# Decoder with routed experts: one shared-expert group ahead of the block loop instead of two, and the token list made behind that group

## The chip, the cores and the metric

The kernel runs on one core of a Trainium2 chip. The metric is the device time of one execution in microseconds (us); lower is better. It is given as the median of several executions.

## What is computed

A two-layer decoder on 16 sequences of 128 tokens and 512 features, in float32. The change lies in its last part alone, the mixture of experts of layer 1, on 2048 tokens (cut from the reference):

```python
scores = softmax(xt @ Wg.T)                    # 16 experts in 4 groups
... top 2 groups by their maximum, then top 4 experts of those: topi, weights
combine = zeros((T, E)).at[arange(T)[:, None], topi].add(weights)
h = silu(einsum('td,eid->eti', xt, W1)) * einsum('td,eid->eti', xt, W3)   # INTER = 352
y = einsum('etd,te->td', einsum('eti,edi->etd', h, W2), combine)
z = silu(xt @ Ws1.T) * (xt @ Ws3.T) @ Ws2.T    # shared expert, 704 wide, for every token
out = _layernorm(x + y + z)
```

## The kernel before

The stage is `build_experts` (from L2088). Its work, in TensorE's order:

1. The tokens are transposed (L2425), router logits are formed (L2431, L2436), and VectorE picks four experts for each token.
2. **Shared groups ahead.** The shared expert z goes by four groups of four sequences (512 tokens). One group is `shared_ups` (six chunks of 128 hidden features, each with a gate tile "sg" and an up tile "su": L2403, 96 matmul records) and then `shared_downs` (four tiles "sy" of 12 records: L2416, 48 records). ScalarE makes the gate (L2370), VectorE the product `hs` (`shared_hidden`, L2610), and VectorE adds the four results to y (`shared_add`, L2617). Groups 0 and 1 (`EARLY`) run here. In the middle of group 0 two small products give each pair of token and expert its rank (L2445, L2446), and VectorE computes the slots from it.
3. **The token list.** 80 slots of blocks hold 128 tokens each, one expert to a block. For each of a token's four choices k, VectorE writes one-hot marks (`mark(k)`, L2671, L2674 and twice L2677) into one of two buffers (`at_row` lies in `back`, `at_block` in the weight buffer of expert 1). TensorE multiplies them (`list_products`, L2454, 16 products for each k, all added up in one bank). `mark(2)` and `mark(3)` write over the buffers of k = 0 and k = 1, and so wait for `list_taken`, which the products of k = 0 and k = 1 raise. `list_out` (L2686 to L2693) turns the bank into token numbers: after its first copy it raises `list_taken` to 4, for which SyncE waits before it loads the weights of expert 1 (L2261, L2262), and its last instruction lets GpSimd copy one column of numbers (L2316) and gather the 128 token rows of block 0 and then of block 1 by an indirect DMA (L2319).
   In the kernel before, the marks of k = 0 and 1 are made by VectorE during the downs of group 0; their products stand behind chunk 2 of group 1, those of k = 2 and 3 behind chunk 4 of it.
4. **The block loop.** TensorE first waits until all early shared results are added (`s_added`) and the rows of block 0 are there (`gathered`), transposes them (`turn(0)`, L2473), and then runs 79 blocks: transpose, gate product (L2483), hidden transpose (L2478), up product (L2483), down product (L2490). ScalarE's `yrow` is stored to DRAM.
5. **Shared groups behind.** Groups 2 and 3 (`LATE`) follow the loop. Beside them GpSimd gathers the 64 tiles of expert results (four for each of 16 sequences, L2335) and VectorE adds them up, weighted (`combine_one`, L2752): up to five behind each chunk's `hs` and one behind each `shared_add`. The normalisation's sums (`sums`, L2760) of sequences 0 to 11 are made in `combine_one` when the fourth result of a sequence is added; `moments_of(0)` follows chunk 3 of the last group, and sequences 0 to 11 are normalised between the additions of the last group (L2771), then the last four.

Each engine runs its instructions strictly in this written order. `Tiles` hands out the eight PSUM banks in the order of the list `order`; a tile can start once the tile eight places earlier has been read.

Of the kernel before, what the change touches and what calls it, by code (L numbers as in the profile page):

```python
# [31 lines left out]
GB = SEQS // GROUPS  # L32
# [2057 lines left out]
def build_experts(nc, t, chunk_in, home):  # L2090
# [10 lines left out]
    with ExitStack() as ctx:  # L2101
# [9 lines left out]
        NGR, TOPG, TOPK = 4, 2, 4  # L2111
# [6 lines left out]
        NI, NS = len(inner), len(shared)  # L2118
# [117 lines left out]
                "sy": lambda: (s_added, GB * n[0] + n[1] + 1),  # L2236
            }[kind]()

        EARLY, LATE = (0, 1), (2, 3)
        early = shared_tiles(EARLY)  # L2240
        RANK_AT = NS // 2
        TURNED = [*range(GB, SEQS), *range(1, GB), 0]
        ROUTED = [*range(1, GROUPS), 0]
        order = [("xt", b) for b in TURNED] + [("rl", g) for g in ROUTED] + [("rt",)]
        LISTED = {2: (0, 1), 4: (2, 3)}
        list_at = early.index(("sg", EARLY[1], min(LISTED) + 1))
        order += early[:2 * RANK_AT] + [("rank",)] + early[2 * RANK_AT:list_at] + [("list",)] + early[list_at:]

        READY = (range(0, SEQS - GB), range(SEQS - GB, SEQS))
        first = Tiles(banks, semaphore("filled"), order, drained)  # L2250
# [146 lines left out]
        def _(pe):  # L2397
# [9 lines left out]
            def shared_ups(tiles, g, chunks=range(NS)):  # L2407
                for c in chunks:
                    up(tiles, ("sg", g, c), ws1, shared[c], g)
                    up(tiles, ("su", g, c), ws3, shared[c], g)  # L2410

            def shared_downs(tiles, g):
                for b in range(GB):
                    bank = tiles.start(pe, 0, ("sy", g, b), [(s_h, NS * (g + 1))])
                    for c in range(NS):
                        ins = pe.matmul(bank[:, :], hs[:, c, b * P:(b + 1) * P], ws2[:, c, :],  # L2416
                                        start=(c == 0), stop=(c == NS - 1))
                    tiles.done(ins)
# [31 lines left out]
            def list_products(ks):  # L2450
                for k in ks:
                    pe.wait_ge(list_marked.sem, k + 1)
                    for b in range(SEQS):
                        ins = pe.matmul(bank[:, 0:2 * LIST], at_row[:, k % 2, b, :],  # L2454
                                        at_block[:, k % 2, b].rearrange("p i j -> p (i j)"),
                                        start=(k == 0 and b == 0), stop=(k == TOPK - 1 and b == SEQS - 1))
                    if k < TOPK - 1:
                        ins.then_inc(list_taken.sem, 1)
                    else:
                        first.done(ins)  # L2460

            for c in range(NS):
                shared_ups(first, EARLY[1], range(c, c + 1))
                if c in LISTED:
                    if 0 in LISTED[c]:
                        bank = first.start(pe, 0, ("list",))
                    list_products(LISTED[c])
            shared_downs(first, EARLY[1])

            def turn(v):  # L2470

# [69 lines left out]
        def _(dve):  # L2541
# [64 lines left out]
            def shared_hidden(tiles, g, c):  # L2606
                n, m = NS * g + c, shared[c][1]
                bank = tiles.wait(dve, 0, ("su", g, c))
                dve.wait_ge(s_gated.sem, n + 1)
                dve.tensor_tensor(hs[0:m, c, :], bank[0:m, :], gated[0:m, n % 2, :], ALU.mult).then_inc(s_h.sem, 1)  # L2610

            def shared_add(tiles, g, b):
                bank = tiles.wait(dve, 0, ("sy", g, b))
                s = GB * g + b
                if s in added:
                    dve.wait_ge(added[s][0].sem, added[s][1])
                dve.tensor_tensor(y[:, s, :], bank[:, :], y[:, s, :], ALU.add).then_inc(s_added.sem, 1)  # L2617
                added[s] = (s_added, s + 1)
# [48 lines left out]
            def mark(k):  # L2667

                if k >= 2:
                    dve.wait_ge(list_taken.sem, k - 1)  # L2670
                vstep.did(dve.tensor_tensor(at_row[:, k % 2], restf[:, k, :].unsqueeze(2).broadcast_to([P, SEQS, P]),  # L2671
                                            columns_of.unsqueeze(1).broadcast_to([P, SEQS, P]), ALU.is_equal))
                one = at_block[:, k % 2, :, 0, :]
                chained(dve.tensor_tensor(one, quotf[:, k, :].unsqueeze(2).broadcast_to([P, SEQS, LIST]),  # L2674
                                          columns_of[:, 0:LIST].unsqueeze(1).broadcast_to([P, SEQS, LIST]), ALU.is_equal))
                for i in (1, 0):
                    ins = dve.tensor_tensor(at_block[:, k % 2, :, i, :], one,  # L2677
                                            marks[:, i, :].unsqueeze(2).broadcast_to([P, SEQS, LIST]), ALU.mult)
                    if i:
                        chained(ins)  # L2680
                ins.then_inc(list_marked.sem, 1)
# [15 lines left out]
            dve.sem_inc(hid_ready.sem, AHEAD)  # L2697
            for c in range(RANK_AT, NS):
                shared_hidden(first, EARLY[0], c)
            for k in LISTED[2]:  # L2700
                mark(k)
            for b in range(GB):
                shared_add(first, EARLY[0], b)
            for c in range(3):
                shared_hidden(first, EARLY[1], c)
            for k in LISTED[4]:
                mark(k)
            for c in range(3, 5):
                shared_hidden(first, EARLY[1], c)
            list_out()  # L2710
            for c in range(5, NS):
                shared_hidden(first, EARLY[1], c)
            for b in range(GB):
                shared_add(first, EARLY[1], b)

            def columns(v):

# [29 lines left out]
            def combine_one():  # L2747
                n, b, k = combine.pop(0)
                dve.wait_ge(returned[n % SLOTS].sem, 16 * (n // SLOTS + 1))
                if b in added:  # L2750
                    dve.wait_ge(added[b][0].sem, added[b][1])
                add_to_y(b, dve.scalar_tensor_tensor(y[:, b, :], back[:, n % SLOTS], top[:, b, k:k + 1], y[:, b, :],  # L2752
                                                     ALU.mult, ALU.add))
                if b in READY[0] and k == TOPK - 1:
                    sums(b)

            def sums(b):

                dve.wait_ge(added[b][0].sem, added[b][1])
                vstep.did(dve.bn_stats(stats[:, b, :], y[:, b, :]))  # L2760
# [13 lines left out]
            for g in LATE:  # L2774
                for c in range(NS):
                    shared_hidden(last, g, c)
                    for _ in range(min(5, len(combine))):
                        combine_one()
                    if g == LATE[-1] and c == NS - 3:
                        moments_of(0)  # L2780
                for b in range(GB):
                    shared_add(last, g, b)
                    if combine:
                        combine_one()
                    if g == LATE[-1]:
                        normalise(0, READY[0][b * len(READY[0]) // GB:(b + 1) * len(READY[0]) // GB])
# [144 lines left out]
```

## Time and profile before

| | us |
|---|---|
| median of 3 runs | 2826.8 (2824.01 to 2828.55) |
| profiled execution | 2823.79, its span 2822.0 |
| TensorE busy in the span | 2639.3 (94%) |
| experts stage begins (first record of L2425) | 1880.5 |
| last TensorE record ends | 2811.4 |

Times below count from the start of the profiled span. A row of the timeline or the chain gives start, duration, engine, line and what is written from what. For TensorE one float32 product of the program leaves two matmul records.

### The profile page before, as it was taken

The numbers are of one execution on the slowest core, as the hardware profiler recorded it, in microseconds if no ns is written. First come the engines' busy times: TensorE is split into PE (matmuls) and PEld (weight loads), VectorE is DVE, ScalarE is ACT, GpSimd is POOL, SyncE is SP. The second block draws the span as 40 slices with busy tenths as digits, with TensorE's granted clock in tenths as the row PEclk, the third lists the DMA queues.
The fourth block names the chain that finished last, engine by engine and source line by source line (L and its number), as shares of the span: only waits on it lengthen the run. The fifth ranks groups of instructions, "written<-read, shape, count | busy, mean of one in ns | idle before, by whom it ended". The sixth has DMA issues, their size and how long they took to land. (4 is left out here: it accounts for less than half of the span.)

```text
span 2822.0 us, 33590 instructions
## 1 busy us (share of the span) xinstructions
PE 2639.3 (94%) x10940; PEld 1330.5 (47%) x10941; DVE 1388.7 (49%) x2555; ACT 839.3 (30%) x1896; POOL 527.3 (19%) x564
## 2 busy tenths in 40 slices
PE   8999999999999958799999999859999999999998
PEld 4544554555465433344344344224456656665543
DVE  4546564564557262567777777607322222222255
ACT  2324332442342232145455455530011111111101
POOL 2111101110111001333233233000011111111054
PEclk9999999999999988899999999979999999999999
DMA  6120122122202301434454454340123333332155
GB/s 197 60 75 30 66 70 90 60 63 86 76 31 75 116 1 61 79 75 104 106 112 103 105 116 98 100 168 0 43 95 130 129 128 126 113 144 97 53 145 160
DMA packets 108316, 260.04 MB, mean 92 GB/s; under 512 B 19523, under 2 KB 53059, under 8 KB 96675
## 3 DMA queue, kind: packets, MB, share of 16 engines
q1 hardware_dynamic: 95490, 219.87, 26.2%
q0 software_dynamic: 11440, 37.50, 4.5%
q8 instruction: 71, 1.16, 0.2%
q10 hardware_dynamic: 1264, 1.10, 0.1%
q14 instruction: 51, 0.41, 0.1%
HBM read 203.14 MB, written 54.89 MB: 91 GB/s over the span
## 5 line engine op out<-in xcount | busy, mean ns | idle before, releaser
L2483 PE MATMUL d_bank<-d_w,d_xcol 128*128 x1264 | 401.3, 461 | 0.0
L2019 DVE TENSOR_REDUCE c_mx<-c_pair 128x2 f32<-128x1024 f32 x256 | 303.5, 1217 | 109.3 <-PE c_pair L1879 108.3
L1728 ACT ACTIVATE c_probs<-c_exp 128x512 f32<-128x512 f32 x512 | 277.9, 597 | 217.0 <-PE c_exp L1893 213.8
L2483 PEld LDWEIGHTS d_bank<-d_w,d_xcol 128*128 128x128 f32 x1264 | 229.0, 191 | 101.0 <-issue 1.4
L796 PE MATMUL a_bank<-h_quarters,a_ring 128*128 128x512 f32 x608 | 272.9, 600 | 0.0
L547 POOL TENSOR_TENSOR a_ry<-a_rt 128x512 f32<-128x512 f32 x80 | 130.3, 1629 | 759.6 <-DVE a_rt L1048 759.6
L796 PE MATMUL a_bank<-a_wo,h_rows 128*128 128x512 f32 x512 | 222.4, 593 | 0.0
L2490 PE MATMUL d_bank<-d_w,d_hid 128*128 x480 | 219.2, 593 | 0.7 <-DVE d_hid L2721 0.7
L1851 PE MATMUL c_step<-h_quarters,c_xT 128*128 128x512 f32 x384 | 185.7, 608 | 7.9 <-DVE c_r L2012 3.8
L1893 PE MATMUL c_exp<-c_qs,c_ks 128*128 128x512 bf16 x512 | 160.5, 384 | 19.5 <-ACT c_probs L1728 11.6
L796 PEld LDWEIGHTS a_bank<-h_quarters,a_ring 128*128 128x128 f32 x608 | 115.0, 193 | 132.3 <-issue 129.6
L2403 PE MATMUL d_bank<-d_xT,d_ws 128*128 128x512 f32 (+1 forms) x384 | 166.7, 594 | 0.7 <-ACT d_yrow L2380 0.7
L2380 ACT ACTIVATE d_yrow<-d_bank 128x512 f32<-128x512 f32 x80 | 47.8, 597 | 380.1 <-PE d_bank L2490 380.1
L796 PEld LDWEIGHTS a_bank<-a_wo,h_rows 128*128 128x128 f32 x512 | 97.4, 190 | 120.9 <-issue 120.4
L2718 DVE COPY d_xcol<-d_bank 128x512 f32<-128x512 f32 x79 | 54.6, 691 | 188.8 <-PE d_bank L2473 188.8
L1879 PE MATMUL c_pair<-c_ks,c_qs 96*128 96x512 bf16 x512 | 142.8, 384 | 3.5 <-DVE c_mx L2019 3.4
L1903 PE MATMUL c_pv<-c_probs,c_vt 128*32 128x512 f32 x1024 | 138.0, 611 | 0.7 <-ACT c_probs L1728 0.7
L2490 PEld LDWEIGHTS d_bank<-d_w,d_hid 128*128 128x128 f32 x480 | 91.3, 190 | 94.0 <-issue 76.4
L585 ACT ACTIVATE a_ee<-a_ry 128x512 f32<-128x512 f32 x80 | 50.8, 635 | 272.3 <-POOL a_ry L547 272.3
L2316 POOL COPY d_index<-d_tokens 128x1 uint32 (+1 forms) x79 | 14.3, 181 | 614.2 <-DVE d_xcol L2718 488.2
L2721 DVE COPY d_hid<-d_bank 128x384 f32<-128x384 f32 x80 | 44.6, 558 | 164.5 <-PE d_bank L2478 164.5
L1851 PEld LDWEIGHTS c_step<-h_quarters,c_xT 128*128 128x128 f32 x384 | 69.5, 191 | 102.2 <-issue 96.0
(305 smaller groups left out, 3559.6 us busy)
## 6 DMA issues: line engine op xcount, KB each, us to landing
d_w<-in_w SPq DMA_DIRECT2D x16, 1408.0 KB
scratch_results<-d_yrow SPq DMA_DIRECT2D x80, 256.0 KB
a_ring<-in_wq SPq DMA_DIRECT2D x16, 1024.0 KB, 4.8
a_wo<-in_wo SPq DMA_DIRECT2D x16, 1024.0 KB, 4.8
c_ks<-scratch_kpark SPq DMA_DIRECT2D x96, 128.0 KB, 4.3
c_qs<-scratch_qpark SPq DMA_DIRECT2D x96, 128.0 KB, 4.3
d_w<-in_w SPq DMA_DIRECT2D x16, 768.0 KB
a_ring<-in_w SPq DMA_DIRECT2D x8, 1024.0 KB, 7.9
```

The lines of the kernel that those rows point to most:

```text
L547: pool.tensor_tensor(ry[:, n % 2, :], rt1[:, n % 2, :], rt2[:, n % 2, :], ALU.add).then_inc(rope_sum.sem, 1)
L796: ins = pe.matmul(bank[:, :], lhs(c), rhs(c), start=(c == 0), stop=(c == n - 1))
L1728: act.activation(probs[:, (LC * CH * n + k) % RING, :], bank[:, :], ACT.Exp, scale=float(CD) ** -0.5).then_inc(exped.sem, 1)
L1851: ins = pe.matmul(bank[:, :], rows[:, c, :], w[:, c, :], start=(c == 0), stop=(c == KC - 1))
L1879: ins = pe.matmul(bank[:, 512 * i:512 * i + 512], qs[0:TR, n % STACKS, h, at0:at0 + P], ks[0:TR, n % STACKS, h, :], start=True, stop=True)
L1893: exps.done(pe.matmul(bank[:, :], ks[:, n % STACKS, h, l * P:(l + 1) * P], qs[:, n % STACKS, h, :], start=True, stop=True))
L1903: ins = pe.matmul(pv[32 * j:32 * j + 32, :], head_values(n, q, l, j), probs[:, (LC * CH * n + QUAD * m + j) % RING, :], start=(l == 0), st ...
L2019: dve.tensor_reduce(mx[:, n % 2, at0:at0 + 2], bank[:, :].rearrange("p (i n) -> p i n", i=2), AX.X, ALU.max).then_inc(maxed.sem, 1)
L2403: ins = pe.matmul(bank[0:m, :], w[:, c, c0:c0 + m], xT[:, c, GT * group:GT * (group + 1)], start=(c == 0), stop=(c == KC - 1))
L2483: ins = pe.matmul(bank[:, 0:FI], xcol[:, v, k, :], w13[:, bass.ds(at, 1), which, k, :].rearrange("p a n -> p (a n)"), start=(k == 0), stop ...
L2490: ins = pe.matmul(bank[:, :], hid[:, v, c * P:(c + 1) * P], w2[:, bass.ds(at, 1), c, :].rearrange("p a n -> p (a n)"), start=(c == 0), sto ...
L2718: dve.tensor_copy(xcol[:, v].rearrange("p c n -> p (c n)"), turned_bank[:, :]).then_inc(xcol_ready.sem, 1)
```

## The change

`EARLY` becomes group 0 alone and `LATE` becomes groups 1, 2 and 3. TensorE makes all four `list_products` in a row, directly behind the downs of group 0. VectorE makes the four marks in a row as well, with the additions of group 0's results behind marks 2 and 3 and behind `list_out`. The sums of sequences 0 to 11 leave `combine_one` and are made in the last late group, four sequences behind each of its first three chunks.

```diff
-        EARLY, LATE = (0, 1), (2, 3)
+        EARLY, LATE = (0,), (1, 2, 3)
...
-        LISTED = {2: (0, 1), 4: (2, 3)}
-        list_at = early.index(("sg", EARLY[1], min(LISTED) + 1))
-        order += early[:2 * RANK_AT] + [("rank",)] + early[2 * RANK_AT:list_at] + [("list",)] + early[list_at:]
+        order += early[:2 * RANK_AT] + [("rank",)] + early[2 * RANK_AT:] + [("list",)]
...
-            for c in range(NS):
-                shared_ups(first, EARLY[1], range(c, c + 1))
-                if c in LISTED:
-                    if 0 in LISTED[c]:
-                        bank = first.start(pe, 0, ("list",))
-                    list_products(LISTED[c])
-            shared_downs(first, EARLY[1])
+            bank = first.start(pe, 0, ("list",))
+            list_products(range(TOPK))
...
-            for k in LISTED[2]:
-                mark(k)
             for b in range(GB):
+                mark(b)
+                if b >= 2:
+                    shared_add(first, EARLY[0], b - 2)
+            list_out()
+            for b in range(2, GB):
                 shared_add(first, EARLY[0], b)
-            for c in range(3):
-                shared_hidden(first, EARLY[1], c)
-            for k in LISTED[4]:
-                mark(k)
-            for c in range(3, 5):
-                shared_hidden(first, EARLY[1], c)
-            list_out()
-            for c in range(5, NS):
-                shared_hidden(first, EARLY[1], c)
-            for b in range(GB):
-                shared_add(first, EARLY[1], b)
...
-                if b in READY[0] and k == TOPK - 1:
-                    sums(b)
...
+                    if g == LATE[-1] and c < NS - 3:
+                        for b in range(GB * c, GB * c + GB):
+                            sums(b)
```

## Rows read from the trace of the kernel before

**Rows 1.** The chain that ended last, around the early groups: start, us, what.
```profile
1948.11 20.87 PE d_bank L2416 x48
1968.97 20.60 PE d_bank L2403 x48
1989.57 2.30 PE d_bank L2454 x32
2005.65 2.30 PE d_bank L2454 x32
2036.63 0.70 DVE h_quarters L2617
2037.38 0.67 PE d_bank L2473 x4
2041.04 1.11 PE d_bank L2473 x4
2042.15 3.41 PE d_bank L2483 x8
...
2050.83 0.44 PE d_bank L2473 x4
...
2058.91 0.44 PE d_bank L2473 x4
```

**Rows 2.** TensorE's timeline behind the block loop.
```profile
2684.94 41.61 PE L2403 MATMUL d_bank<-d_xT,d_ws 128*128 128x512 f32 x96 [0.69 <-ACT d_yrow L2380]
2727.48 20.87 PE L2416 MATMUL d_bank<-h_rows,d_hs 128*128 128x512 f32 x48 [0.93 <-DVE d_hs L2610]
2748.19 41.51 PE L2403 MATMUL d_bank<-d_xT,d_ws 128*128 128x512 f32 x96
2790.54 20.87 PE L2416 MATMUL d_bank<-h_rows,d_hs 128*128 128x512 f32 x48 [0.84 <-DVE d_hs L2610]
```

**Rows 3.** VectorE's timeline: marks 0 and 2, next mark, additions, `list_out`.
```profile
1947.98 2.27 DVE L2671 TENSOR_TENSOR d_back<-d_restf,d_spots 128x2048 bf16<-128x2048 f32 x1
...
1961.38 1.28 DVE L2617 TENSOR_TENSOR h_quarters<-d_bank,h_quarters 128x512 f32<-128x512 f32 x2
...
1990.76 2.29 DVE L2671 TENSOR_TENSOR d_back<-d_restf,d_spots 128x2048 bf16<-128x2048 f32 x1 [0.46 <-PE d_bank L2454]
...
1994.51 3.05 DVE L2677 TENSOR_TENSOR d_w<-d_w,d_spots 128x1296 bf16<-128x1296 bf16 x2
1997.48 2.28 DVE L2671 TENSOR_TENSOR d_back<-d_restf,d_spots 128x2048 bf16<-128x2048 f32 x1
...
2007.98 0.69 DVE L2610 TENSOR_TENSOR d_hs<-d_bank,d_gated 128x512 f32<-128x512 f32 x1 [3.11 <-PE d_bank L2454]
2008.59 0.32 DVE L2686 COPY d_listed<-d_bank 128x162 f32<-128x162 f32 x1
```

**Rows 4.** The timeline of GpSimd and of SyncE's queue at the token list.
```profile
2008.99 0.34 SPq L2261 DMA_DIRECT2D d_w<-in_w  x1
...
2011.33 1.15 POOL L2319 DMA_INDIRECT d_xrow<-scratch_x,d_index  x1 [0.91 <-POOL d_index L2316]
```

**Rows 5.** The gathers of token rows: all 79, then the first alone.
```profile
DMA to landing us min/median/max: 3.2/3.4/7.8
...
DMA to landing us min/median/max: 6.1/6.1/6.1
```

**Rows 6.** Stretches: us, busy time of each engine, granted clock, DMA share, GB/s.
```profile
1870.00:1880.00 10.00, 0.00 (x0) 0.00 (x0) 2.98 (x7) 0.50 (x2) 0.00 (x0) 0.50 0.14 54
2040.00:2042.00 2.00, 0.96 (x5) 0.96 (x6) 0.00 (x0) 0.00 (x0) 0.95 (x1) 0.68 0.19 41
2042.00:2044.00 2.00, 2.00 (x5) 1.25 (x5) 0.69 (x1) 0.00 (x0) 0.18 (x1) 0.50 0.25 90
2044.00:2046.00 2.00, 2.00 (x9) 1.28 (x9) 0.07 (x1) 0.31 (x1) 0.97 (x1) 0.97 0.07 12
2016.00:2017.00 1.00, 1.00 (x3) 0.41 (x3) 0.00 (x0) 0.00 (x0) 0.00 (x0) 1.00 1.01 399
```

**Rows 7.** VectorE's timeline at the end: last combination, closing sums, normalisation.
```profile
2795.78 0.75 DVE L2752 SCALAR_TENSOR_TENSOR h_quarters<-d_back,d_top,h_quarters 128x512 f32<-128x512 f32 x1 [0.55 <-DMA d_back<-scratch_results,d_row_no]
...
2813.41 2.46 DVE L2760 BATCH_NORM_STATS2 d_stats<-h_quarters 128x6 f32<-128x512 f32 x4
...
2816.89 1.91 DVE L2771 TENSOR_SCALAR h_quarters<-h_quarters,d_mom,d_rstd 128x512 f32<-128x512 f32 x4 [0.60 <-ACT d_rstd L2359]
```

## The prediction

> **What bounds the kernel now.** I read the busy times, then the chain of work that ended last in the experts stage, then the timelines of the engines around it. The reader should see in the chain [rows 1] that from the downs of group 0 (1948.11) to the first block nearly every piece is TensorE's, each starting where the last one ends. The token list costs TensorE only its two runs of products (2.30 us each); all that VectorE, GpSimd and the DMA do for it lies beside group 1. Behind the loop [rows 2] it is the same: from 2684.94 TensorE stands still only for 0.93 and 0.84 us, ahead of the downs. So a shared group costs about its TensorE time wherever it stands, and the question is what it covers there. Ahead of the loop it covers the making of the token list. Behind the loop it covers the 64 combinations, and those are covered with two groups already: the last one starts at 2795.78 [rows 7], and TensorE works until 2811.4 [rows 2].
>
> **What is moved at no cost or gain.** The products, marks, additions, gathers and weight loads are the same in number before and after. Group 1 leaves the front with the TensorE time that it brings to the back. The sums of 12 sequences leave the combinations and come, four at a time, behind three chunks of the last group, where the combinations are now finished: the combinations need 64 places, 34 of which (6 x 5 + 4) are in the first late group and 30 in the second. Four sums are 2.46 us [rows 7], and a chunk's TensorE time is 41.5/6 = 6.9 us [rows 2], which hides them; without that cover the 12 would cost 7.4 us. VectorE is freer by as much in the first two late groups, and the two waits of 0.93 and 0.84 us may shrink to the 0.77 us that hs alone needs (41.61 from 2684.94 to 2726.55 is followed by one hs of 0.69 and two handovers): at most 0.2 us, taken as nothing. The end is the same chain as before: last downs, last addition, four sums, moments, normalisation, 10.6 us from TensorE's end to 2822.0. The third late group doesn't touch it, because these four sequences belong to the last group in both kernels.
>
> **What is added at the back.** One more group. The distance from one late group to the next is 2748.19 - 2684.94 = 63.25 us [rows 2], with its wait. TensorE is the bound in it: **+63.25**.
>
> **What is taken from the front.** Before, from the end of the downs of group 0 (1968.97) to turn(0) (2037.38) there are 68.4 us [rows 1]. They go. In their place stands the list's own chain, now bare. I follow it step by step.
> - TensorE starts the products of k = 0 at 1968.97. The products stand behind the downs in its order, though marks 0 and 1 have been ready since 1961.4 [rows 3].
> - VectorE stands at mark(2), which waits for the buffer of k = 0. Queued behind it are the additions of group 0, mark(3) and list_out, and all of GpSimd's and SyncE's next work waits for those. Before, mark(2) began 1.19 us after the products began (1989.57 to 1990.76) [rows 1, 3]. So it begins at 1970.16.
> - A mark takes 6.72 us to the next start (1990.76 to 1997.48), 6.80 to the end of its last part (1994.51 + 3.05) [rows 3]. Behind mark(2) comes one addition, half of the distance that two took (0.6 to 0.65 us; 0.60 taken). mark(3) then begins at 1977.48 and ends at 1984.28. Products of k = 2 run beside it.
> - TensorE has been idle from 1971.3 but for the products of k = 2. In the idle stretch 1870 to 1880 the granted clock was 0.50, that is the level of 1.2 GHz; at 2040 to 2042, after four microseconds with almost nothing since 2036.6, it was falling (0.68), and at 2042 to 2044, with work again, 0.50 [rows 6]. So the products of k = 3 are taken at half speed: 16 of the 32 that took 2.30 us are 1.15 at the full clock, 2.30 at half [rows 1]. With the handover list_out starts at 1986.66. At the full clock it would be 1985.5.
> - From list_out's first copy (2008.59) to the start of the first gather (2011.33) were 2.74 us, and the gather landed 6.1 us after that (2017.43) [rows 3 to 5]: 8.84 us together. So block 0 is there at 1995.50. Additions 2 and 3 (1.3 us) are done beside this.
> - The landing needs a choice. The median gather took 3.4 us, the longest 7.8 [rows 5]. The first was issued 2.34 us after the load of expert 1 (2008.99) [rows 4], and while it was under way the DMA engines were fully busy (1.01, 399 GB/s) [rows 6]. The change keeps load and gather in the same order and distance, so I take 6.1 and keep 3.4 and 7.8 for the range.
> - On that last point the Trainium skill ("DMA: Bandwidth & Descriptors", section "Issuing engines are not separate DMA queues") says that DMAs issued by SyncE and by GpSimd run on the same 16 engines and interleave. The trace agrees: 6.1 beside the full load, 3.4 as the median. By queues of their own the sum would be 2.7 us lower.
>
> turn(0) begins at about 1995.54, where it began at 2037.38: **-41.84**. It runs at the low clock: 1.11 against 0.67 us, as the transposes at 2041.04 [rows 1], **+0.44**. From turn(0) to the next transposes were 3.66 us before, most of it loop entry; block 1 lands close behind block 0 and doesn't hold them. The first products of the loop were slow before too (3.41 against 2.37), behind a pause of 4 us, so nothing more is added for them. The upper bound is a first block wholly at half speed: blocks are 8.08 us apart (2050.83 to 2058.91), the first took 9.79 (2041.04 to 2050.83) [rows 1], and twice 8.08 is 6.4 more than that.
>
> **Sum.** 63.25 - 41.84 + 0.44 = **+21.85 us**. The same from the other side: TensorE is idle from 1971.3 to 1995.5, 24.2 us, less 2 or 3 us of products within, less the 0.8 us that it stood before turn(0) before, plus the slow pieces. On the profiled execution 2823.79 + 21.85 = 2845.6. The median of the three runs is 3.0 us above the profiled execution, so for a median I take 2826.8 + 21.85 = **2848.7 us**, 0.8% slower.
>
> **The rivals.**
> - *The gather isn't hindered, or the clock holds.* A landing of 3.4 instead of 6.1 is -2.7, the products at full clock -1.15, turn(0) at full clock -0.44: 2844.4. Against it: rows 5 and 6.
> - *The chain is longer.* A gather of 7.8 (+1.7) and a first block wholly at the lower clock (+6.4): 2856.8. For it: the pause is 24 us instead of 5, and nothing in this stage shows one so long ahead of the loop. Against it: at 2044 to 2046 the granted clock is back at 0.97 after some 3 us of work.
> - *The change doesn't leave mark(2) waiting*, the four marks run through under the downs of group 0, as "in a row" would have it. Then the marks end at 1947.98 + 4 x 6.7 + 0.6 = 1975.4 instead of 1984.3: 2839.8. Against it: mark(2) waits for products that TensorE has behind the downs, so the order in the code excludes it. It would need products earlier in the queue.
> - *Not slower: the stream of results back (GpSimd's gathers and VectorE's combinations) is the bound behind the loop*, not TensorE. Then the third group fills time that is there anyway, its 63.25 us aren't paid, and only the -41.4 of the front is left: about 2785. The chain of waits does pass through GpSimd and DMA between 2695 and 2727, which speaks for it. Against it: the stream is done at 2796.5, 111.6 us after 2684.94, and two groups of TensorE alone are 126.5. It decides from the point at which the stream is longer than the TensorE time beside it: for a sum of zero 22 of the 63 us would have to be hidden, so it would have to end 22 us or more behind the two groups, and it ends 15 us ahead.
>
> **How the numbers follow.** Forecast 0.78; unhindered gather or full clock 0.07; longer chain 0.09; marks without a wait 0.02; stream as the bound 0.02; 0.02 for what none of these names. The range runs from the second case's 2844.4, less most of the spread of the executions (the lowest lay 2.8 us under the median), up to the larger of the third's two parts, 2848.7 + 6.4 = 2855.1: 2842.0 to 2855.0. A measurement of this kernel can tell about 0.2% (5.7 us) from no change. Slower by more than that needs +5.7, and every case but the stream gives +13 or more: slower 0.96, within 0.2% 0.02, faster 0.02.
>
> **What would show it.** In the profile after: products of L2454 in one stretch directly behind the first 48 records of L2416, with two pauses in which VectorE's L2671, L2674 and L2677 run (mark(2) beginning near 1970.2, mark(3) near 1977.5); list_out near 1986.7; a first L2473 near 1995.5; granted clock 0.5 in between; three late groups at a distance of 63.2 us, and 10.6 us from TensorE's end to the span's. The prediction is wrong if TensorE's pause ahead of turn(0) isn't 20 to 26 us in all, or if the third late group costs less than its 63 us, which would mean that something other than TensorE was the bound behind the loop.

## The result: 0.6% slower

| | before | changed |
|---|---|---|
| median of 4 runs | 2826.31 us | 2844.81 us (2840.32 to 2846.01) |
| ratio, with its 95% interval | | 1.0064 (1.005 to 1.0079) |
| profiled execution, its span | 2823.79, 2822.0 | 2845.80, 2844.0 |

The forecast was 2848.7 us, in a range of 2842 to 2855. In the profile after, L2401 is the line of the shared ups, L2414 of the downs, L2452 of the list products, L2466 of the token transposes and L2476 of the gate and up products. The marks are L2664, L2667 and L2670, `list_out` begins at L2679.

The chain that ended last in the changed kernel, from the downs of group 0 to the second block (start, us, what). It answers to [rows 1].

```profile
1947.48 20.87 PE d_bank L2414 x48
1968.35 1.16 PE d_bank L2452 x16
1969.51 0.02 issue
1969.53 2.29 DVE d_back L2664
...
1976.34 0.60 DVE h_quarters L2610
1976.93 2.20 DVE d_back L2664
...
1982.13 1.52 DVE d_w L2670
1983.66 0.05 issue
1983.70 2.36 PE d_bank L2452 x16
1986.06 0.02 issue
1986.08 0.34 DVE d_listed L2679
...
1988.83 5.83 DMA d_xrow<-scratch_x,d_index
1994.66 0.14 issue
1994.80 1.10 PE d_bank L2466 x4
...
1998.87 1.11 PE d_bank L2466 x4
1999.98 4.40 PE d_bank L2476 x8
...
2009.65 0.44 PE d_bank L2466 x4
```

Where [rows 1] showed TensorE without a break, the chain now leaves it for VectorE (marks of k = 2 and 3), comes back for one run of products, and goes out again through `list_out` and the gather's DMA. The stretch from the end of the downs (1968.35) to turn(0) (1994.80) is 26.45 us; before it was 68.4 us, with group 1 in it.

TensorE's waits in the experts stage of the changed kernel (who waited for whom: us in total, times, longest):

```profile
PE d_bank L2452 <- DVE d_w L2670: 10.7, 2, 5.8
PE d_bank L2466 <- DMA d_xrow<-scratch_x,d_index: 8.8, 1, 8.8
```

These two rows don't exist before the change. They are 19.5 us of TensorE standing still. The two pauses for the marks, in TensorE's timeline (the first row of products, those of k = 0 and 1, begins at 1968.18 without a wait):

```profile
1976.39 2.34 PE L2452 MATMUL d_bank<-d_w,d_back 128*128 128x162 bf16 x16 [5.75 <-DVE d_w L2670]
1983.70 2.34 PE L2452 MATMUL d_bank<-d_w,d_back 128*128 128x162 bf16 x16 [4.97 <-DVE d_w L2670]
```

TensorE's timeline behind the loop of the changed kernel, which answers to [rows 2]:

```profile
2643.76 41.61 PE L2401 MATMUL d_bank<-d_xT,d_ws 128*128 128x512 f32 x96 [0.69 <-ACT d_yrow L2378]
2686.57 20.87 PE L2414 MATMUL d_bank<-h_rows,d_hs 128*128 128x512 f32 x48 [1.20 <-DVE d_hs L2603]
2707.28 41.51 PE L2401 MATMUL d_bank<-d_xT,d_ws 128*128 128x512 f32 x96
...
2770.26 41.51 PE L2401 MATMUL d_bank<-d_xT,d_ws 128*128 128x512 f32 x96
```

Three groups at distances of 63.52 and 62.98 us. Within them TensorE waits only ahead of the downs (1.20, 0.78 and 0.78 us). The last TensorE record ends at 2833.4, and the span 10.6 us later, as before.

**A measure that is finer than the whole time.** The executions of one kernel spread by 5 to 16 us, and the layers ahead of the experts alone spread by 14: in the 13 profiles of this study the first shared products start anywhere from 1895.6 to 1910.0, with the same instructions ahead of them. The experts stage repeats much better: 939.77 and 939.03 us in two profiles of the changed kernel, and A and B of the kernel before came out the same to 0.01 us in e5, whose edit touches only C. One part of B repeats less well, the first block (see below). So the experiments are read by three stretches of their profiled executions: A from the first shared products to turn(0), B from turn(0) to the first late group (the loop), and C from there to the end of the span.

| kernel | A | B | C | sum | against before | median | ratio to before, 95% interval |
|---|---|---|---|---|---|---|---|
| before | 132.52 | 647.56 | 137.06 | 917.14 | | 2826.31 | |
| changed | 90.57 | 648.96 | 200.24 | 939.77 | +22.6 | 2844.81 | 1.0064 (1.005 to 1.0079) |
| e0 changed, once more | 90.67 | 648.35 | 200.01 | 939.03 | +21.9 | 2848.22 | 1.0077 (1.0062 to 1.0092) |
| e1 buffer for each mark | 80.91 | 648.62 | 199.98 | 929.51 | +12.4 | 2836.15 | 1.0034 (1.0022 to 1.0047) |
| e2 load behind gathers | 88.21 | 648.27 | 199.85 | 936.33 | +19.2 | 2844.84 | 1.0062 (1.0047 to 1.0078) |
| e3 filler products | 89.69 | 646.04 | 200.26 | 935.99 | +18.9 | 2844.66 | 1.0065 (1.0049 to 1.0081) |
| e9 = e1 and e2 | 79.18 | 648.88 | 200.16 | 928.22 | +11.1 | 2834.73 | 1.0032 (1.0021 to 1.0044) |
| e4 list early, sums moved | 147.14 | 648.82 | 143.32 | 939.28 | +22.1 | 2843.37 | 1.0072 (1.0054 to 1.009) |
| e5 sums moved alone | 132.52 | 647.57 | 142.53 | 922.62 | +5.5 | 2828.63 | 1.0019 (1.0008 to 1.0031) |
| e10 list early alone | 147.01 | 648.77 | 136.79 | 932.57 | +15.4 | 2833.99 | 1.005 (1.0034 to 1.0066) |
| e6 one late group | 195.50 | 648.43 | 122.01 | 965.94 | +48.8 | 2872.17 | 1.018 (1.0159 to 1.0201) |
| e7 late wait | 130.83 | 647.75 | 135.14 | 913.72 | -3.4 | 2820.11 | 0.9983 (0.9972 to 0.9994) |
| e8 late wait, turn(0) early | 133.47 | 642.40 | 135.15 | 911.02 | -6.1 | 2817.81 | 0.9973 (0.9962 to 0.9984) |

(In e8 A ends at turn(1), since turn(0) stands inside the downs; by the same mark the kernel before has A 136.18 and B 643.90. Each ratio is to runs of the kernel before made beside that kernel; their medians were 2821.7 to 2827.7 us. The edits shift the lines of the program, so each profile's rows carry the line numbers of its own kernel.)

### The profile page after: what moved, and what is told of

It is laid out like the page before. It is cut to its first block and busy times, and to the rows that moved or that the text cites. A ratio compares the mean times of both kernels' runs of the same rounds, so it can differ in the third digit from the quotient of the medians.

```text
span 2844.0 us, 33531 instructions
## 1 busy us (share of the span) xinstructions
PE 2634.7 (93%) x10881; PEld 1330.1 (47%) x10941; DVE 1386.2 (49%) x2555; ACT 838.6 (29%) x1896; POOL 528.7 (19%) x564
## 3 DMA queue, kind: packets, MB, share of 16 engines
q8 instruction: 71, 1.16, 0.2%
## 5 line engine op out<-in xcount | busy, mean ns | idle before, releaser
L2476 PE MATMUL d_bank<-d_w,d_xcol 128*128 x1264 | 402.2, 461 | 0.0
L2476 PEld LDWEIGHTS d_bank<-d_w,d_xcol 128*128 128x128 f32 x1264 | 229.0, 191 | 101.6 <-issue 2.0
L1893 PE MATMUL c_exp<-c_qs,c_ks 128*128 128x512 bf16 x453 | 147.2, 383 | 26.6 <-ACT c_probs L1728 12.3
L2401 PE MATMUL d_bank<-d_xT,d_ws 128*128 128x512 f32 (+1 forms) x384 | 166.4, 593 | 0.7 <-ACT d_yrow L2378 0.7
```

The costliest lines, as they stand in the source:

```text
L1893: exps.done(pe.matmul(bank[:, :], ks[:, n % STACKS, h, l * P:(l + 1) * P], qs[:, n % STACKS, h, :], start=True, stop=True))
L2401: ins = pe.matmul(bank[0:m, :], w[:, c, c0:c0 + m], xT[:, c, GT * group:GT * (group + 1)], start=(c == 0), stop=(c == KC - 1))
L2476: ins = pe.matmul(bank[:, 0:FI], xcol[:, v, k, :], w13[:, bass.ds(at, 1), which, k, :].rearrange("p a n -> p (a n)"), start=(k == 0), stop ...
```

## The experiments

Two theories were set against each other. A: the cost is the token list's chain, which now stands bare in front of TensorE. B: the cost lies behind the loop, where a third group stands beside the stream of results back. (The letters of the theories have nothing to do with those of the stretches.)

**e0, the base.**

> The changed kernel once more, beside the three variants of it on the same chip, as their base. Expected 1.0064 of the kernel before again (about 2844.5 us), and in the profile some 26.5 us from the end of the downs of group 0 to turn(0).

Measured: 1.0077, and 26.6 us from the end of the downs of group 0 to turn(0) (1967.09 to 1993.64). The changed kernel repeats itself; its median here, 2848.2 us, is 3.7 above the one expected, and the two intervals overlap.

**e1, a buffer for each mark.**

```diff
-                if k >= 2:
-                    dve.wait_ge(list_taken.sem, k - 1)
-                one = at_block[:, k % 2, :, 0, :]
+                one = at_blocks[k][:, :, 0, :]
...
+        at_rows = [at_row[:, 0], at_row[:, 1], row_more[0], row_more[1]]
+        at_blocks = [at_block[:, 0], at_block[:, 1], block_third, block_more]
```

> The changed kernel with a buffer of its own for each of the four marks (k = 2 in yrow and in expert 1's down weights, k = 3 in xrow and in new memory), so mark(2) no longer waits for the products behind the downs. Theory A (the cost of the change is the token list's chain, bare in front of TensorE): marks 2 and 3 run through under the downs, mark(3) ends near 1974.9 instead of 1983.7 in the profile (-8.8 us), and the products of k = 3 meet TensorE after a pause of only 3 us, so perhaps at the full clock (-1.2 us): 2834 to 2836 us, turn(0) near 1985. Theory B (the cost lies behind the loop, where a third group stands beside the stream of results back, and the front's pause only hides in it): a shorter front moves the end by less than 2 us: 2843 to 2845 us.

TensorE's timeline of e1 behind the downs of group 0:

```profile
1968.75 2.46 PE L2459 MATMUL d_bank<-d_w,d_back 128*128 128x162 bf16 x32
1971.05 1.31 PE L2459 MATMUL d_bank<-d_w,d_yrow 128*128 128x162 bf16 x16
1975.48 1.32 PE L2459 MATMUL d_bank<-d_block_more,d_xrow 128*128 128x162 bf16 x16 [3.12 <-DVE d_block_more L2675]
1985.70 1.09 PE L2473 MATMUL d_bank<-h_ident,d_xrow 128*128 128x128 f32 x4 [8.90 <-DMA d_xrow<-scratch_x,d_index]
```

Two pauses of 5.75 and 4.97 us have become one of 3.12, and the last products run at full speed (1.32 instead of 2.34). A falls by 9.76 us against e0 and the sum by 9.5: what the front gains arrives at the end. B and C stay. The median shows it too: 2836.2 us, where theory A had 2834 to 2836 and theory B 2843 to 2845. That speaks for theory A, and against B, by which the end would not have moved.

**e2, the load of expert 1 held back.**

```diff
             sp.wait_ge(expert_in.sem, 32)
+            for v in range(2):
+                sp.wait_ge(gathered[v].sem, 16)
             load_expert(sp, 1, 1)
```

> The changed kernel with the load of expert 1 held back until the first two gathers of token rows have landed; nothing else is changed. If the load is what makes the first gather take 5.8 us instead of the usual 3.4: landing at 3.4, turn(0) 2.4 us earlier, about 2842 us (-2.4). If the first gather is slow for a reason of its own: still 5.8 us and no gain. Theory B: no gain in either case.

The landing of the first gather, first in the changed kernel, then in e2:

```profile
DMA to landing us min/median/max: 5.8/5.8/5.8
...
DMA to landing us min/median/max: 3.5/3.5/3.5
```

A falls by 2.46 us against e0. The load is what slowed the gather. The median expected, about 2842 us, was not reached (2844.8): the gain is too small for the whole time to show it (1.0062 against 1.0077, with overlapping intervals). The trace shows it at its place. In e9 it is found once more.

**e3, filler products in TensorE's pauses.** The 24 products go to a bank that nobody reads, so the output doesn't change.

```diff
+            def filler(n):
+                for _ in range(n):
+                    pe.matmul(banks[7][:, :], xT[:, 0, 0:P], xT[:, 0, 0:GT], start=True, stop=True)
-            list_products(range(TOPK))
+            list_products(range(2))
+            filler(6)
+            list_products(range(2, 3))
+            filler(6)
+            list_products(range(3, 4))
+            filler(10)
...
             turn(0)
+            filler(2)
```

> The changed kernel with 24 float32 products that nobody reads, in TensorE's pauses: 6 ahead of the products of k = 2, 6 ahead of those of k = 3, 10 ahead of turn(0), 2 behind it. If the lower granted clock is what makes the pieces behind the pauses slow: products of k = 3 at 1.16 instead of 2.36 us, turn(0) and turn(1) at 0.44 instead of 1.10, the first gate product at 2.37 instead of 4.40, together -4.6 us, less up to 1 us for the two products behind turn(0): 2840 to 2841.5 us. If those pieces are slow for another reason (first run of the code, weights): 2844.5 or a little more.

The chain of e3:

```profile
1982.78 1.33 PE d_bank L2452 x16
...
1993.00 0.63 PE d_bank L2475 x4
...
1996.60 0.65 PE d_bank L2475 x4
1997.25 2.40 PE d_bank L2485 x8
```

Each piece that was slow behind a pause is fast: 1.33 for 2.36, 0.63 for 1.10, 0.65 for 1.11, 2.40 for 4.40. (L2475 are the transposes and L2485 the gate product here.) The granted clock of e3 is 1.00 in every stretch of 2 us from 1966 to 2006. The sum falls by 3.0 us against e0, less than the 3.6 to 4.6 expected. e0's first gate product took 3.62, not the 4.40 that the expectation used, which is 0.8 of the difference. The median, 2844.7 us, taken by itself fits the second case of the expectation (2844.5) and not the first (2840 to 2841.5). But e0 beside it ran to 2848.2, and the intervals of the two overlap, so the reading rests on the rows alone.

So about 3 us of the changed kernel's time are the lower clock's. Not all of that is part of the change's price, since the kernel before runs the same transposes of block 1 and the same gate product slowly too (1.11 and 3.41 us, [rows 1]). What the change adds by the clock is the products of k = 3 (1.03 us) and turn(0) (0.43), 1.5 of the 22 us.

**e4, the list early with two groups ahead.**

```diff
-        EARLY, LATE = (0,), (1, 2, 3)
+        EARLY, LATE = (0, 1), (2, 3)
...
             list_products(range(TOPK))
+            shared_ups(first, EARLY[1])
+            shared_downs(first, EARLY[1])
```

> One half of the change: marks in a row and all products directly behind the downs of group 0, as in the changed kernel, but groups 0 and 1 both ahead of the loop and 2 and 3 behind it, as before; list_out, the gathers and the load of expert 1 lie beside group 1. Theory A (bare list chain): only the two pauses for marks 2 and 3 are paid, 5.75 + 4.97 us, the products of k = 2 and 3 at the lower clock, 2.4 us, and 1.5 to 2 us because group 1 begins at it: +14.5 to +15 us, of the changed kernel's +22; from the start of group 0's downs to the end of the span 888.5 us (before 873.9, changed 895.8 to 896.5). Theory B (the cost lies in the third late group): 873.9, no change.

A is 14.6 us longer than before, as theory A had it. But the sum is +22.1, not +15: C is 6.3 us longer too, with the same two late groups as before. Theory B had no change at all and falls as well. That the sum comes out close to the changed kernel's 22.6 is a coincidence. What is different in C is only the place of the sums, which e5 tests.

**e5, the sums alone.**

```diff
-                if b in READY[0] and k == TOPK - 1:
-                    sums(b)
...
                     for _ in range(min(5, len(combine))):
                         combine_one()
+                    if g == LATE[-1] and c < NS - 3:
+                        for b in range(GB * c, GB * c + GB):
+                            sums(b)
```

> The other small part alone: the kernel before with the sums of sequences 0 to 11 moved from the combinations to the first three chunks of the last group. My forecast took it as nothing: within 0.3 us of before in the stretch from the start of group 0's downs to the end of the span (873.9 us). If VectorE's place in the combinations mattered: the two waits ahead of the late downs (0.93 and 0.84 us) fall or rise by some tenths.

My expectation fell: C grows by 5.5 us (142.53 against 137.06). VectorE's timeline in the last group of e5:

```profile
2746.49 0.69 DVE L2610 TENSOR_TENSOR d_hs<-d_bank,d_gated 128x512 f32<-128x512 f32 x1 [5.51 <-PE d_bank L2403]
2747.10 3.12 DVE L2752 SCALAR_TENSOR_TENSOR h_quarters<-d_back,d_top,h_quarters 128x512 f32<-128x512 f32 x4
2751.93 0.75 DVE L2752 SCALAR_TENSOR_TENSOR h_quarters<-d_back,d_top,h_quarters 128x512 f32<-128x512 f32 x1 [1.71 <-DMA d_back<-scratch_results,d_row_no]
2752.60 2.47 DVE L2758 BATCH_NORM_STATS2 d_stats<-h_quarters 128x6 f32<-128x512 f32 x4
2754.98 0.68 DVE L2610 TENSOR_TENSOR d_hs<-d_bank,d_gated 128x512 f32<-128x512 f32 x1
...
2763.20 0.67 DVE L2610 TENSOR_TENSOR d_hs<-d_bank,d_gated 128x512 f32<-128x512 f32 x1
```

and TensorE's downs behind it:

```profile
2785.39 22.56 PE L2416 MATMUL d_bank<-h_rows,d_hs 128*128 128x512 f32 x48 [4.46 <-DVE d_hs L2610]
```

With two late groups the last one still carries 30 combinations. From one `hs` to the next VectorE needs 8.2 to 8.5 us, and a chunk of TensorE is 6.9, so `hs` comes later with each of the first chunks. VectorE's own work is not too long for the chunk: 1.71 and 1.46 us of those stretches are a wait ahead of the fifth combination, and without it 6.8 are left. The program has four buffers for results (`SLOTS = 4`), so the gather for the fifth starts only when the first combination has read its buffer, and this gather stands in e5's chain: the first combination ends at 2747.86, the gather runs from 2748.11 for 3.79 us, and the fifth combination begins at 2751.93. Four combinations in a row are over before it has landed, and the sums come only behind the fifth. In the kernel before, a sum lies between the combinations and fills a part of this time:

```profile
2757.49 0.69 DVE L2760 BATCH_NORM_STATS2 d_stats<-h_quarters 128x6 f32<-128x512 f32 x1
...
2760.60 0.75 DVE L2752 SCALAR_TENSOR_TENSOR h_quarters<-d_back,d_top,h_quarters 128x512 f32<-128x512 f32 x1 [0.90 <-DMA d_back<-scratch_results,d_row_no]
```

At the end TensorE stands 4.46 us ahead of the last downs instead of 0.84, and those run slower (22.56 against 20.87, at a granted clock of 0.66 from 2785 to 2790): 3.6 and 1.7 of the 5.5 us. In the changed kernel the last group has no combinations, and there four sums between two `hs` leave 3.80 us of idle time:

```profile
2777.94 2.46 DVE L2743 BATCH_NORM_STATS2 d_stats<-h_quarters 128x6 f32<-128x512 f32 x4
2784.20 0.69 DVE L2603 TENSOR_TENSOR d_hs<-d_bank,d_gated 128x512 f32<-128x512 f32 x1 [3.80 <-PE d_bank L2401]
```

So the sums' new place costs nothing with three late groups and 5.5 us with two.

**e10, the list early alone.** e4 with the sums back in `combine_one`.

> The token list made directly behind the downs of group 0, with groups 0 and 1 ahead of the loop, 2 and 3 behind it, and the sums back in the combinations: what e4 was meant to be. In e4 the stretch ahead of turn(0) grew by 14.6 us as expected, but the stretch behind the loop grew by 6.3 us too, and moving the sums alone (e5) cost 5.5 us from the first ups of group 0 to the end (922.6 against 917.1 us). If that is the sums' doing: the late groups take 137 us again (before 137.06, e4 143.3), and the whole stretch from the first ups to the end is 917.1 + 14.6 + up to 1.3 for a slower first block = 931.8 to 933 us. If the list's place makes the late groups slower: 939 us again.

C is 136.79, as before, and the sum +15.4. This separates the two: the list's place costs 14.5 us in A and nothing in C. B is 1.2 us longer, and that is the first gate product of the loop, 4.60 us in e10's chain for the 3.41 of [rows 1]. In e10's timeline, where each record reaches a little into the one before it:

```profile
2049.91 1.11 PE L2469 MATMUL d_bank<-h_ident,d_xrow 128*128 128x128 f32 x4 [3.01 <-issue]
2050.81 4.81 PE L2479 MATMUL d_bank<-d_w,d_xcol 128*128 x8
```

This is not a price of the list's place: TensorE's pauses just ahead of it are the same as before (0.78 us ahead of turn(0), 3.0 behind it), and e7 and e6, with those pauses and the list where it was before, took 3.86 and 4.30 us for the same product.

**e6, the opposite: one late group.** Groups 0, 1 and 2 ahead of the loop; sequences 0 to 11 are normalised behind the last combination.

```diff
-        EARLY, LATE = (0, 1), (2, 3)
+        EARLY, LATE = (0, 1, 2), (3,)
...
             while combine:
                 combine_one()
+            moments_of(0)
+            normalise(0, READY[0])
```

> The opposite of the change: groups 0, 1 and 2 ahead of the loop, 3 alone behind it; the moments of sequences 0 to 11 and their normalisation behind the last combination, because the sums need it. It asks how much TensorE time the stream of results back needs as cover. If the stream is as long as it was before (111.6 us from the start of the late groups to the last combination), the end comes some 14 us behind it, at 126 us instead of 137, with 63 us more ahead of the loop: +46 (if the stream runs faster with less beside it, 105 us) to +52 us, 2873 to 2880 us. If the stream were short and TensorE's time all that counts: about +4 us, for the 12 sequences normalised behind the end.

Measured: +48.8 us, as a stretch within the +46 to +52 expected; the median, 2872.2 us, is 0.8 under the 2873 to 2880. C is 122.0 us although TensorE has 63 us less to do in it. From the start of the late group (2739.49) to the end of the last combination (2845.98) are 106.5 us, a little less than the 111.6 before. So the stream of results back needs some 107 to 112 us of TensorE's time as cover. Two groups (126.5) give it; one (some 63) doesn't; a third gives nothing more.

**e9, e1 and e2 together.**

> The changed kernel with both shortenings of the bare chain, a buffer for each mark and the load of expert 1 behind the first two gathers. From the start of group 0's downs to the end of the span the first alone gave 886.3 us and the second alone 893.1, against 895.8 of the changed kernel beside them. If the two lie one behind the other in one chain, they add up: 883.6 us, about 2833 us. If they overlap: 886.

928.2 us instead of 883.6 + 43.2 = 926.8 us for the same stretch counted from the first shared products: the two lie in one chain and add up but for 1.4 us. Of these 0.7 is the products of k = 3 (2.03 us here, 1.32 in e1, both behind a pause of 3.1 us). Where the clock stands behind a pause of 3 us isn't the same in every execution. The rest, 0.3 us in B and 0.3 in C, is no more than these stretches differ by between the profiles of the changed kernel.

**e7 and e8, a version that beats both.** This one was built on the kernel before. Its profile shows four stops of TensorE ahead of the downs and the pauses at the entry of the loop. e7 lets the first tile of the downs wait for the sixth `hs` only ahead of its sixth product:

```diff
-                    bank = tiles.start(pe, 0, ("sy", g, b), [(s_h, NS * (g + 1))])
+                    bank = tiles.start(pe, 0, ("sy", g, b), [(s_h, NS * (g + 1) - (b == 0))])
                     for c in range(NS):
+                        if b == 0 and c == NS - 1:
+                            pe.wait_ge(s_h.sem, NS * (g + 1))
```

> The kernel before; the first tile of each group's downs no longer waits for all six hidden chunks but for five, and for the sixth ahead of its sixth product. TensorE's four stops of 0.77 to 0.93 us ahead of the downs should go, since five products are 4.3 us and hs needs 0.7: -3.1 to -3.3 us, 870.6 us from the start of group 0's downs (which comes 0.8 us earlier) to the end counted from the last record of the ups before it; median about 2823.3. If the combinations on VectorE hold hs for longer behind the loop, a part of the two late stops stays.

e8 puts turn(0) and its copy behind the second downs tile of group 1 as well:

```diff
                 for b in range(GB):
+                    if g == EARLY[-1] and b == 2:
+                        pe.wait_ge(gathered[0].sem, 16)
+                        turn(0)
...
             for b in range(GB):
                 shared_add(first, EARLY[1], b)
+                if b == 1:
+                    dve.wait_ge(filled.sem, turned(0))
+                    columns(0)
```

> As the one before, and turn(0) and its copy stand in the middle of group 1's downs, where the rows of block 0 have long landed. TensorE's pause ahead of the loop loses turn(0)'s handovers (-1.4 us), and if it is then too short for the granted clock to fall, the first block runs at the full one (-1.7 us): -4.6 to -6.4 us in all against before, 2820 to 2822 us. If the loop's entry needs turn(0) to be late for another reason (the next gather starts with its copy), only the -3.2 us stay.

The chain of e8 at the loop's entry, to be laid beside [rows 1]:

```profile
2034.21 0.70 DVE h_quarters L2620
2034.91 2.24 issue
2037.15 0.65 PE d_bank L2415 x4
2037.80 2.37 PE d_bank L2488 x8
...
2045.44 0.44 PE d_bank L2415 x4
```

e7 gives -3.4 us and 0.9983 (0.9972 to 0.9994): the four stops are gone from TensorE's waits. e8 gives -6.1 us and 0.9973 (0.9962 to 0.9984), the fastest kernel of the study by its stretches; the intervals of e7 and e8 overlap. (In this profile L2415 are the transposes and L2488 the gate product.) Its pause ahead of the loop is a single one of 3 us, and the granted clock stays at 1.00 from 2034 to 2042, where the kernel before falls to 0.50. The first block's gate products take 2.37 us instead of 3.41, and the block 8.29 us (2037.15 to 2045.44) instead of 9.79. Both medians came out lower than expected (2820.1 for about 2823.3, 2817.8 for 2820 to 2822), while the stretches lie at or near the expected -3.1 to -3.3 and within -4.6 to -6.4.

## Why the prediction was right

**The mechanism.** TensorE bounds both ends of the stage, so the moved group costs its own time at either place, and the change strips the list's chain of its cover. C grew by 63.18 us for a group of 63.25. e1 and e2 show the bare chain: what is taken off it comes off the end. e10 shows that the early place of the list costs 14.5 us even with the groups where they were. e6 shows the limit: with one late group it is no longer TensorE that bounds the end.

**The terms.**

| term | forecast | measured in the profile |
|---|---|---|
| front: turn(0) against the downs of group 0 | -41.84 | -41.95 (A: 90.57 - 132.52) |
| loop: turn(0) and first block at the lower clock | +0.44 | +1.40 (B) |
| back: one more group | +63.25 | +63.18 (C) |
| sum | +21.85 | +22.63 |
| span of the whole execution | +21.85 | +22.0 |

The single steps held as well. The times between the end of the downs and each step were, forecast and measured: mark(2) begins 1.19 and 1.18 us behind it, mark(3) 8.5 and 8.5 (1976.85 in VectorE's timeline), list_out 17.69 and 17.73, turn(0) 26.57 and 26.45. The gather took 5.83, not 6.1. The products of k = 3 took 2.36 us for the 2.30 assumed.

**A sign of being wrong that was drawn too narrowly.** The prediction called itself wrong if TensorE's pause ahead of turn(0) "isn't 20 to 26 us in all". From the end of the products of k = 1 (1970.65, two runs of 1.16 us behind 1968.35) to turn(0) are 24.2 us, which is the figure that it named. But the time in which TensorE stood still is 19.5 us (5.75, 4.97 and 8.75), just outside. The sum taken from the other side subtracted "2 or 3 us of products within"; the two runs, both at the lower clock, took 4.7. The forecast's own steps had the products of k = 3 at 2.30 us, and with k = 2 the same its 24.2 leave 19.6. So it is this second sum and the bound of 20 drawn from it that were wrong, and not the chain.

**What the sum had too small: the first block.** I took its slow products as the same before and after. They weren't: the first gate product took 4.40 us (3.41 before), and the block 10.78 us (1998.87 to 2009.65) for 9.79. The granted clock of the changed kernel at this place (us, busy time of each engine, clock, DMA):

```profile
1972.00:1974.00 2.00, 0.00 (x0) 0.00 (x0) 1.97 (x2) 0.00 (x0) 0.00 (x0) 0.81 0.00 0
1974.00:1976.00 2.00, 0.00 (x0) 0.00 (x0) 1.97 (x2) 0.00 (x0) 0.00 (x0) 0.50 0.00 0
...
2002.00:2004.00 2.00, 2.00 (x5) 1.13 (x4) 0.00 (x0) 0.00 (x0) 0.91 (x1) 0.51 0.17 39
2004.00:2006.00 2.00, 2.00 (x10) 1.34 (x9) 0.56 (x1) 0.46 (x1) 0.00 (x0) 1.00 0.26 92
```

It is at 0.50 from 1974 until 2004, five us after TensorE has steady work (1998.87). Before it came back three us after (2041.04 to 2044, [rows 6]). In e3, where the clock stays at 1.00, the slow pieces are fast.

It would be wrong to read from this that the longer pause makes the first block slower. How late the clock comes back isn't fixed. With the pauses of the kernel before (0.78 and 3.0 us, one at each side of turn(0)) the same gate product took 3.41 us before, 3.42 in e5, 3.86 in e7, 4.30 in e6, 4.60 in e10 and 4.66 in e4. Behind the long wait for the gather it took 4.40 us in the changed kernel, 3.62 in e0, 4.06 in e1, 3.53 in e2 and 4.30 in e9. The two lists cover the same range, with means of 4.04 and 3.98. So only the 0.43 us of turn(0) are the change's (1.10 us for 0.67 in all of these), as forecast, and the other 1.0 lies within what this product varies by anyway: the 3.41 of the kernel before is the lowest of the eleven.

**What was right only in its place: the sums at no cost.** The forecast said that the combinations are finished by then, and that without this cover the 12 sums would cost 7.4 us, their own time. e5 measures 5.5 us where the combinations aren't finished, but not for that reason: the sums' own time would have fitted, and what they cost came of standing behind the wait for the fifth result. I then wrote an expectation for e5 as if they were free there too, and it missed, because the condition (no combinations in the last group) doesn't hold with two late groups.

**The whole time.** The forecast for the median was 3.9 us too high although the profile's sum was right to 0.2 us (2845.6 forecast, 2845.80 measured). That the profile was hit so closely is in part luck: the stage grew by 0.8 us more than forecast, and the two profiled executions happened to reach it 0.6 us apart, where the 13 profiles lie up to 14 us apart. The medians differ by 18.5 us, and by 20.5 in e0's runs, where the stage differs by 22.6 and 21.9; the interval of the ratio, 1.005 to 1.0079, is 14 to 22 us. The spread of the layers ahead of the stage is large enough for the difference, but that it is the cause isn't shown: in nine of the twelve kernels the ratio lies 0.5 to 4.5 us below what the stretches give, and above it in one.

**The rivals.** The measured median, 2844.8 us, lies nearer to the 2844.4 of the first rival than to the forecast, and the median alone can't tell them apart. The trace does: the gather took 5.83 us and not 3.4, the products of k = 3 took 2.36 and not 1.15, turn(0) 1.10 and not 0.67. e2 shows that it is the load that hinders the gather. The longer chain did not come: the gather was no slower than before, and the first block took 1.0 us more and not 6.4. Also ruled out are marks without a wait, by the pauses of 5.75 and 4.97 us. The stream as the bound is ruled out by the distances of the late groups, and e6 shows where it would begin: somewhere between one group and two.

## What to carry to other kernels

Work that is independent of everything isn't free to move: ask what it covers where it stands. Here one group of 63 us covered a chain of 26 us ahead of the loop and nothing behind it, since two groups already gave the 107 to 112 us that the stream back needs. Before an instruction is moved "to a quiet place", lay down what its engine does between two deadlines there, waits included, and on which side of a wait the instruction comes to stand: the sums were free in one kernel and cost 5.5 us in its near twin, where they stood behind a wait that they had partly filled before. And when a chain must be bare, look at what is queued beside it: a buffer of its own for each step was worth 9.5 us, holding back a load that nobody waited for 2.5 us. Before a microsecond of difference is put down to a change, see how much the same piece varies in kernels that the change didn't touch there: the first block's gate product ran from 3.41 to 4.66 us.

## What the runs showed of the hardware

- The first gather of 128 rows landed 5.8 to 6.2 us after its issue in the eleven profiles with a load of 2.2 MB under way, and 3.5 and 3.6 us in the two without it (e2, e9). The Trainium skill says in "DMA: Bandwidth & Descriptors", section "Issuing engines are not separate DMA queues", that DMAs started by different engines run on the same 16 engines and interleave. The trace agrees: load and gather are issued by SyncE and GpSimd, and without the load the gather landed 2.3 to 2.7 us sooner.
- Products behind a pause of TensorE of 3.1 us ran at full speed in one execution (1.32 us for 16) and partly at half in another (2.03). Behind the pauses of 5.75 and 4.97 us they took 2.34 or 2.35 in all five profiles that have them (changed, e0, e2, e4, e10; the chain's rows give up to 2.36). Products that nobody reads, put into the pauses, kept the granted clock up and gave 3 us back.
- A stop of only 4.5 us ahead of the last downs cost another 1.7 us in them (22.56 against 20.87), and one of 4.14 us in e4 2.8 us (23.70).
- The first gate product of the loop (2.37 us at the full clock) took 3.4 to 4.7 us in eleven profiles, whether TensorE's pauses around turn(0) were under 4 us together or 9 to 12. It was fast only in e8, with one pause of 3 us, and in e3, with filler products.
